# Layer-1 attention pass of a graph network: the second half of each block's value sums stands behind the maxima, and the key-and-value gathers wait half by half

## The reference, cut to what matters

```python
q = (x @ Wq + bq).reshape(n, H, C)          # H = 8 heads, C = 32
k = (x @ Wk + bk).reshape(n, H, C)
v = (x @ Wv + bv).reshape(n, H, C)
e = (edge_attr @ We).reshape(-1, H, C)
k_j = k[src] + e
v_j = v[src] + e
alpha = jnp.sum(q[dst] * k_j, axis=-1) / jnp.sqrt(jnp.float32(C))
amax = jax.ops.segment_max(alpha, dst, num_segments=n)
ex = jnp.exp(alpha - amax[dst])
denom = jax.ops.segment_sum(ex, dst, num_segments=n)
out = jax.ops.segment_sum(v_j * (ex / denom[dst])[:, :, None], dst, num_segments=n)
```

## Time and profile before

| what | value |
|---|---|
| runs of the kernel before | 5891.51, 5898.32, 5899.26 us, median 5898.32 us |
| the profiled execution | 5889.27 us, its span 5887.5 us |
| busy over the span: PE, DVE, ACT, POOL | 49%, 65%, 24%, 57% |
| layer-1 pass, weighing instruction L1152 | 98 times, first start 3762.8 us, last 5353.4 us |
| DMA in the pass | 321 GB/s on average |

### The profile page before, as it was taken

The page is one execution under the profiler, slowest core; times in us unless marked ns, Lnnn a source line. Parts: engine busy times, 40 slices in busy tenths (PEclk is TensorE's granted clock), DMA queues, the critical chain, the costliest instruction groups (busy, mean ns, idle before and its releaser), DMA issues. The chain is left out here.

```text
span 5887.5 us, 49851 instructions
## 1 busy us (share of the span) xinstructions
PE 2894.1 (49%) x13052; PEld 2231.5 (38%) x13052; DVE 3811.9 (65%) x6117; ACT 1441.5 (24%) x2526; POOL 3381.2 (57%) x3382
## 2 busy tenths in 40 slices
PE   7513200000000000036888858588888888885777
PEld 5412200000000000035555523477777777774456
DVE  7357778885555545456332345599999999995763
ACT  1123323331333333211222211122222222221320
POOL 0267767777777777572320246677777777773200
PEclk9655555555555555565999979799999999996888
DMA  3033353332353333233321224799999999994113
GB/s 97 35 94 106 106 175 106 107 108 78 108 214 107 107 112 111 85 100 113 102 86 55 85 95 176 243 324 324 324 324 323 324 324 324 324 324 134 64 50 138
DMA packets 289926, 961.77 MB, mean 163 GB/s; under 512 B 79009, under 2 KB 119592, under 8 KB 248229
## 3 DMA queue, kind: packets, MB, share of 16 engines
q0 software_dynamic: 171296, 483.60, 27.2%
q1 hardware_dynamic: 118484, 476.59, 24.3%
HBM read 626.03 MB, written 345.69 MB: 165 GB/s over the span
## 5 line engine op out<-in xcount | busy, mean ns | idle before, releaser
L1235 PE MATMUL e_psE<-e_we,e_eaT 128*128 128x256 f32 x3136 | 900.0, 413 | 266.1 <-DVE e_wv L1134 142.3
L1097 POOL DMA_INDIRECT e_kv<-kv,rec x784 | 875.4, 1117 | 267.4 <-issue 238.5
L765 POOL DMA_INDIRECT g_g<-t,rec x784 | 775.0, 989 | 278.4 <-issue 278.1
L765 POOL DMA_INDIRECT g_g<-t,dst_of x784 | 743.3, 948 | 259.3 <-issue 257.5
L1235 PEld LDWEIGHTS e_psE<-e_we,e_eaT 128*128 128x128 f32 x3136 | 646.8, 209 | 387.0 <-ACT e_eaT L1178 286.3
L1393 PE MATMUL j_psM<-ident,tail 128*128 128x128 f32 x32 | 7.5, 429 | 1150.0 <-PEq L53 1150.0
L1236 PE MATMUL e_psE<-e_kv,ident 128*128 128x256 f32 x1568 | 507.9, 408 | 0.0
L802 DVE TENSOR_TENSOR_SCAN g_wv<-g_fx,g_wv 128x2176 f32<-128x2176 f32 x98 | 459.0, 4683 | 0.4 <-issue 0.4
L1393 PEld LDWEIGHTS j_psM<-ident,tail 128*128 128x128 f32 x32 | 7.0, 330 | 1150.8 <-issue 1150.8
L1104 POOL DMA_INDIRECT e_q<-q,q_of x392 | 370.6, 945 | 119.4 <-issue 119.4
L942 ACT ACTIVATE g_st<-g_wv 128x2048 f32<-128x2048 f32 x98 | 375.9, 3836 | 0.0
(11 more groups left out here) (513 smaller groups left out, 6546.1 us busy)
## 6 DMA issues: line engine op xcount, KB each, us to landing
state<-e_st SPq DMA_DIRECT2D x98, 1088.0 KB
e_ea<-in_edge_attr SPq DMA_DIRECT2D x98, 896.0 KB, 9.4
state_f<-g_st SPq DMA_DIRECT2D x49, 1088.0 KB, 4.3
state_b<-g_st SPq DMA_DIRECT2D x49, 1088.0 KB, 4.2
m_work<-xs SPq DMA_DIRECT2D x119, 128.0 KB, 2.2
ys<-m_work SPq DMA_DIRECT2D x119, 128.0 KB, 1.7
xs<-g_ta SPq DMA_DIRECT2D x28, 512.0 KB
g_g<-t,rec POOLq DMA_INDIRECT x784
```

The source lines that it names most:

```text
L765: pool.indirect_dma_start(g[:, u, j, :], None, tab, bass.IndirectOffsetOnAxis(ap=at_, axis=0)).then_inc(gat[u], 16)
L1097: pool.indirect_dma_start(kv[:, u, b, :], None, c.kv, bass.IndirectOffsetOnAxis(ap=c.rec[:, t, 1:2], axis=0)).then_inc(gkv[u][b // 4], 16)
L1235: nc.tensor.matmul(half, eaT[:, m, j, k, :], we[:, k, :], start=(k == 0), stop=False)
```

## The change

Three edits in `edge_pass`. VectorE's value sum for the second half of a block moves from before the reduction to behind the subtraction of the maxima, with a drain after it. VectorE no longer posts `used`. POOL waits ahead of gather 0 and again ahead of gather 4 of a block, each time for the value sum of the half of `kv` that it is about to overwrite, by the semaphore `ed`.

```diff
-        ld, gq0, gq1, eg0, eg1, used, exd, cwd, dnd, std, so0, so1, free, dump, tp, tcp, ep, ed = (
+        ld, gq0, gq1, eg0, eg1, exd, cwd, dnd, std, so0, so1, free, dump, tp, tcp, ep, ed = (
...
-                if blk >= U:
-                    pool.wait_ge(used, blk - U + 1)
-                    c.alone(pool)
                 for b in range(B):
                     t = blk * B + b
+                    if blk >= U and b % 4 == 0:
+                        pool.wait_ge(ed, 4 + 4 * (blk - U) + 2 + b // 2)
+                        c.alone(pool)
...
+                    quads = [psE[:, half * 1024:(half + 1) * 1024] for half in range(2)]
+
+                    def values(half):
+                        tt(wv[:, 4 * half:4 * half + 4, :], kv[:, u, 4 * half:4 * half + 4, D:2 * D],
+                           quads[half].rearrange("p (j n) -> p j n", j=4), ALU.add).then_inc(ed, 2)
+
                     for half in range(2):
-                        quad = psE[:, half * 1024:(half + 1) * 1024]
                         q4 = q[:, u, 2 * half:2 * half + 2, :].rearrange("p m n -> p (m n)")
-                        v4 = kv[:, u, 4 * half:4 * half + 4, D:2 * D]
                         v.wait_ge(ep, blk * 4 + 2 * half + 2)
-                        tt(q4, quad, q4, ALU.mult)
-                        tt(wv[:, 4 * half:4 * half + 4, :], v4, quad.rearrange("p (j n) -> p j n", j=4), ALU.add).then_inc(ed, 2)
+                        tt(q4, quads[half], q4, ALU.mult)
+                        if half == 0:
+                            values(0)
                     v.drain()
-                    v.sem_inc(used, 1)
...
                     tt(ex[:], at[:], top[:], ALU.subtract).then_inc(exd, 1)
+                    values(1)
+                    v.drain()
                     v.wait_ge(cwd, blk + 1)
```

More of the change, by code:

```diff
@@ L1034, in edge_pass @@
         st = sb("st", [P, U, B, SW])
-        ld, gq0, gq1, eg0, eg1, used, exd, cwd, dnd, std, so0, so1, free, dump, tp, tcp, ep, ed = (
-            sem(n) for n in ("ld", "gq0", "gq1", "eg0", "eg1", "used", "exd", "cwd", "dnd", "std", "so0",
+        ld, gq0, gq1, eg0, eg1, exd, cwd, dnd, std, so0, so1, free, dump, tp, tcp, ep, ed = (
+            sem(n) for n in ("ld", "gq0", "gq1", "eg0", "eg1", "exd", "cwd", "dnd", "std", "so0",
                              "so1", "free", "dump", "tp", "tcp", "ep", "ed"))
```

## The result

| | before | after |
|---|---|---|
| median of 5 runs | 5894.58 us | 5951.54 us |
| lowest, highest | 5891.51, 5899.26 | 5940.29, 5956.77 |
| ratio, 95% interval | | 1.0092, 1.0078 to 1.0106 |
| profiled execution | 5889.27 us | 5956.52 us |

The forecast was 5906 us, 8 above the median known then (5898.32) and no change that could be told, with a range up to 5940. Measured were 5951.54 us: 57 us above the kernel before, 45 above the forecast and outside its range.

What follows compares the result with a forecast made beforehand. VectorE's own chain was taken to set the pass's period. Its saving of −22 us and waits of +31 made +9 on the profiled 5889.3 us, 5898, given as 5906 in terms of the median; range 5872 to 5940.

Steps and rivals of the forecast that it cites:

- VectorE's saving: VectorE's chain from product to weighing: 0.22 us a block shorter, −22 us over 98 blocks, between −18 and −27.
- PE's late PSUM half: PE gets the second half's PSUM later, stands still some 0.5 us; five us of reserve hide it, cost 0.
- POOL loses a gather: Between weighings, at a 13.80 us stretch the 11th start is held; POOL falls back one gather in two blocks.
- My own sign: Blocks with under 13.87 us from weighing's end to next weighing, and two gathers stretched over 2 us, show the loss.
- The price of the lost gather: VectorE waits for late keys before its second product: about 0.35 us a block, 88 × 0.35 = +31 us.
- A wait gives the gather back: A VectorE wait lengthens the stretch to the next weighing; from 0.07 us on POOL gets its 12th gather back.
- The mean of both blocks: One block's VectorE wait is the next's reserve, so about half the mean counts: 0.15, 0.33, 0.7 us a block.
- Rival 2: VectorE waits for half-clock keys before its second product, 0.7 to 0.9 us a block: +40, 5938 us; chance 0.20.
- Rival 1: No gather lost at POOL, or waits stay tiny; VectorE's saving alone gives 5876 us (5871 to 5880); chance 0.26.
- Rival 3: DMA is the bound and everything stays: 5898 us; chance 0.08.

Runs made afterwards that it cites:

- e4: Changed kernel with three small sums (result unused) added on VectorE behind the second value sum; 5886.4 us, ratio 0.9992 to the kernel before.
- e5: Changed kernel with the weighing cut into two instructions of half the size; 5865.5 us, ratio 0.9962 to the kernel before.
- e3: Changed kernel with one small sum (result unused) added on VectorE behind the second value sum; 5940.9 us, ratio 1.0074 to the kernel before.
- e9: Kernel before, its sum over the products leaving out the last of a block's eight edges; 5942.6 us, ratio 1.0084 to the kernel before.
- e8: Changed kernel with 24 unused transposes on PE between the two halves of a block's keys; 5919.9 us, ratio 1.0055 to the kernel before.
- e7: Changed kernel loading one in eight attribute rows of partitions 0 to 111 from the third block on; 5911.4 us, ratio 1.0037 to the kernel before.

## Why the forecast was wrong, point by point

- *VectorE's saving.* 0.22 us forecast, 0.18 to 0.28 as bounds, 0.29 measured: product to weighing was 6.18 us and is 4085.98 − 4080.09 = 5.89. Product to reduction came out at 1.29 (1.31), subtraction to value sum at 0.15 (0.15), value sum to weighing at 1.30 (1.36). The drain and the fulfilled wait ahead of the weighing left a gap of 0.09 us (4084.68 + 1.21 to 4085.98), no more than the drain behind the reduction; the forecast had taken 0.15.
- *PE's late PSUM half.* Costs nothing, as forecast: in e4 and e5 VectorE waits 4.6 us for PE in the whole pass.
- *POOL loses a gather.* Right in mechanism and threshold: stretch 13.70 us, the eleventh gather held, in every second block; e3, e4 and e9 show it from both sides. One count in the working slipped: behind the start at E + 1.12 follow ten more up to E + 13.91, not nine, and the 11 starts that it goes on with are right. My own sign for it was put wrongly: I asked for two held gathers in a block. There is still one, of 2.9 us instead of 2.2, and it is the eleventh.
- *The price of the lost gather.* This is the step that failed. "VectorE waits 0 or 0.6 us at the first such place … 0.15, 0.33, 0.7 us a block", and 0.35 taken. Measured: 87.3 us in 98 blocks, 0.89 us a block, waits of 1.4 to 2.3 us in every second block, and that at the first late place (the first long wait, ahead of the seventh weighing, is at once 2.09 us). Where the sum had −22 + 31, the trace has −28 + 84 and the 3 us of lost overlap. Two terms were too small. The eighth gather, issued at E + 6.43 as I had it, let PE start at 4089.96, E + 17.7. I had taken 16.6, and my upper bound was 16.9, by the attributes' landing. And the lower clock cost 2.5 us (7.74 − 5.26), in a half that ends at E + 25.4 against the E + 24.0 at which VectorE wants it. I had let the slow clock come now and then, since the rows of before showed it so, but there PE was idle in one piece ahead of a block; the late gather puts the idleness right ahead of the half that is already late, and all 46 began at the lower clock. The two terms need each other: an estimate from the same rows gives no wait if the half starts at 4089.96 and takes 5.26 us, 0.5 us if it starts at E + 16.6 and takes 7.74, and 1.6 us with both, as measured. e8 takes part of the clock's cost away. e7 takes 32 us away by the ratios, and it isn't separated there how much of that is earlier landing and how much the shorter idleness behind it.
- *A wait gives the gather back.* Right in kind, wrong as a brake. A wait of 0.17 us would keep POOL even, but behind the first weighing the trace has waits of 0.15 us and of 1.36 us and more, and none between. That the lateness comes in steps of one gather is my reading of it; no run varies the step. The kernel settles on 13.70 us with 11 gathers and about 15.9 us with 13.
- *The mean of both blocks.* "About half of the mean counts" was right: the wait of one block is the reserve of the next, 1.8 us in every second.
- *The rivals.* Rival 2 was the case that came, with 40 us for the 57 measured, and 0.20 of the chance. Its condition, that the late half meets the slow clock nearly always, and its price of 0.7 to 0.9 us a block are what the trace shows; the sum took 0.35. Rival 1 was the value of e5, 25 us faster, once the hold was shortened. Rival 3, DMA as the bound, is refuted by e5.

## What to carry to other kernels

Where two engines are both nearly full and one holds up the other's instructions, count the second engine's instructions between two holds before you shorten the first. If the last one only just fits, a saving can cost more than it gives, and a few hundredths of a us decide. Shorten the hold before the stretch: cutting the long instruction in two cost 0.05 us and turned 55 us of loss into 25 us of gain. And when data comes late by a step, price what the waiting engine does afterwards at its lower clock.

## What the runs showed of the hardware

- A gather whose start falls 0.09 to 0.24 us behind the start of the 128x2048 product of two SBUF tiles is held until 0.83 us behind its end (3.02 us in e9, 2.94 in e3 and 2.88 in the changed kernel, instead of 0.95). One that starts 0.03 us behind passes (e4), and the product is 0.06 us longer (2.35 instead of 2.29; at most 2.37 in e4). In these traces the change from one to the other lies at 0.04 to 0.05 us.
- After 3.6 to 5.6 us of idleness PE's next half began at the lower clock 46 times of 46 in the changed kernel (7.74 us instead of 5.26 in the pair shown). In the kernel before, the two blocks of the earlier trace rows that began after 4.2 us of idleness were granted 0.86 and 0.77 on average.
- Less work can be slower: e9 drops 0.27 us of VectorE work a block (the sum takes 2.02 us instead of 2.29) and loses 54 us between the medians.
